# Two-layer transformer block on one core: k turned one head later in layer 0, masks of the maxima moved to VectorE and score pairs in layer 1

## The chip, the cores and the metric

The kernel runs on one core of one Trainium2 chip, in one launch. The metric is the device time in microseconds, the median of several executions. Engines are named as in the profile: PE is TensorE, DVE VectorE, ACT ScalarE, POOL GpSimd, SP SyncE (it issues the transfers).

## What is computed

Two layers follow each other on x of 1024 positions by 512 (32-bit floats). Each has an attention and a feed-forward part, each behind a layer norm with a scale and a shift from a small conditioning vector, and added to x through a gate. The change touches the two attentions. Cut to them:

```
# layer 0: 32 query heads, 8 k/v heads, head size 128, 4-bit weights
q, k, v = [((h @ ((qw - 8) * repeat(scales, 128, axis=0)))) ...]
q, k = q*cos + rotate_half(q)*sin, k*cos + rotate_half(k)*sin
scores = where(causal, q @ k.T / sqrt(128), min)
ctx = softmax(scores) @ v            # k, v of a group serve 4 heads
x += gate * (ctx @ dequantized(w_o))
# layer 1: 32 query heads, 8 k/v heads, head size 16
q, k = rope(q), rope(k)
scores = where(causal, q @ k.T / sqrt(16), -1e20)
x += gate * (softmax(scores) @ v @ w_o.T + b_o)
```

## The kernel before, in words

Constants, sizes: P is 128 partitions, S 1024 positions in NT = 8 tiles, two halves of HALF = 512 (TPH = 4 tiles each). 32-bit products are done on PE as products of a high and a low part in the format fp32r.

**Layer 0's attention** (`layer0_attention_phase`, line 350) goes through 256 units, 32 heads by 8 query tiles. PE's program is one loop over the units: the scores of the next unit, a part of the previous head's output product, partial products of the next head's q and, in every second unit, of the next group's k and v (`kv_partial`), the values, and the transposes of the probabilities. A group is 4 heads on one k and v; REP0 is 4. In a group's first head the partial products of the next group's k for positions 0 to 511 are made, in its second head those for 512 to 1023, then those of v. DVE adds the partial sums, and POOL applies the rotary embedding to each finished sum (`rope`, line 558 on: six instructions in order, the last at line 567 writes the low part). POOL's order is written out by hand (lines 612 to 618, and in the same order the list `pool_ropes`, lines 416 to 423, from which semaphore counts come). In head h: second half of q of head h, the o weights of head h (`make_o`, lines 591 to 600), first half of q of head h+1, and in two of four heads one half of k of the next group. PE waits for q's low part ahead of the first and the fifth query tile of a head, and for k's ahead of a group's first head; k has two places, by group.

The maximum of a row is taken on DVE in one custom instruction (line 768): it adds the table `keys_allowed` (0 or a large negative number) to the scores in PSUM, writes them back negated, and keeps the minimum; it is followed by a read of the accumulator.

**Layer 1's attention** (`layer1_attention_phase`, line 1341) goes by the 8 k/v groups of 4 heads of size 16. High and low parts of q and k lie stacked along the partitions, so one product gives a full-precision score. The scores are made twice. The y scores (queries on the partitions) of the group after only serve the maxima: `score_y` on PE, then `maximum` on DVE (line 1649), a plain maximum over at most 512 keys. The negated maxima are placed into the q stack, so that the x scores (keys on the partitions, `score_x`) come out with them subtracted; ACT takes the exponential (line 1712) into `probsT`, and `values` on PE (line 1583) multiplies with v. A piece on the diagonal is masked by a second, accumulating product of an identity and the bf16 tile `mem.causal` (line 1550 for x, 1569 for y). x has three PSUM banks, y three, the values one, and one bank serves all transposes ("staging": k line 1526, q line 1533, context line 1591), which DVE (k, context) or ACT (q) empties before the next use. A group has 48 x pieces (32 on the diagonal) and 48 y pieces (32 on the diagonal, widths 128, 256, 384 and 512 equally often).

The list `order` (lines 1365 to 1380) sets the program of every engine for one turn: x pieces 0 to 47 of a group, from the eighth on mixed with 6 y pieces of the next group for every 5, staging steps at fixed places, values one step behind. There are seven such turns; ahead of them stands a prologue with only the first group's y and staging steps (`order_first`), behind them the last group's x alone (`order_last`). DVE takes the k transposes of the next group out in two copies for each half (line 1642).

## Time and profile before

| what | value |
|---|---|
| runs | 1892.85, 1895.84, 1897.75 us; median 1895.84 |
| profiled execution, own time | 1891.85 us |
| its span | 1890.1 us |
| mean granted PE clock | 0.97 |
| busy, share of the span | PE 92%, DVE 61%, POOL 47%, ACT 43% |
| layer 0's attention | about 71 to 1044 us of the span |
| layer 1's attention | about 1385 to 1760 us |

The profile records one execution. Busy is the time in which an engine had an instruction under way; what it records of a matmul includes the way through the array, so that neighbours overlap. Idle time is given with what ended it. A timeline row with x2 or more is several like instructions in a row, with the time from the first start to the last end. The granted clock is 1.00 at 2.4 GHz and 0.50 at 1.2 GHz.

### The profile page before, as it was taken

The numbers are of one execution on the slowest core, as the hardware profiler recorded it, in microseconds if no ns is written. First come the engines' busy times: TensorE is split into PE (matmuls) and PEld (weight loads), VectorE is DVE, ScalarE is ACT, GpSimd is POOL, SyncE is SP. The second block draws the span as 40 slices with busy tenths as digits, with TensorE's granted clock in tenths as the row PEclk, the third lists the DMA queues.
The fourth block names the chain that finished last, engine by engine and source line by source line (L and its number), as shares of the span: only waits on it lengthen the run. The fifth ranks groups of instructions, "written<-read, shape, count | busy, mean of one in ns | idle before, by whom it ended". The sixth has DMA issues, their size and how long they took to land. (4 is left out here: it accounts for less than half of the span.)

```text
span 1890.1 us, 25001 instructions
## 1 busy us (share of the span) xinstructions
PE 1730.7 (92%) x9031; PEld 1264.5 (67%) x9031; DVE 1156.7 (61%) x2249; ACT 809.6 (43%) x1780; POOL 885.1 (47%) x784
## 2 busy tenths in 40 slices
PE   5699999999999999999999599998859999999778
PEld 3567777777777776777777388876735555555457
DVE  6856666566666575656655833345787666664475
ACT  3445454545445454545454221100315566566221
POOL 1686786876867868678774400000351222210200
PEclk9899999999999999999999899999879999999989
DMA  5101101010110110100100312102200000000021
GB/s 185 34 28 35 34 18 45 18 45 18 34 37 26 30 33 17 40 28 23 34 12 1 114 52 66 30 1 97 81 1 1 1 1 1 1 1 1 28 44 45
DMA packets 75315, 63.38 MB, mean 34 GB/s; under 512 B 23470, under 2 KB 53358, under 8 KB 75194
## 3 DMA queue, kind: packets, MB, share of 16 engines
q1 hardware_dynamic: 75194, 61.79, 11.0%
q8 instruction: 73, 1.20, 0.3%
q14 instruction: 48, 0.39, 0.1%
HBM read 59.68 MB, written 2.10 MB: 33 GB/s over the span
## 5 line engine op out<-in xcount | busy, mean ns | idle before, releaser
L844 ACT ACTIVATE a_probs<-psum,a_neg_max 128x128 f32<-128x128 f32 (+7 forms) x256 | 190.2, 743 | 265.3 <-DVE a_neg_max L768 265.0
L768 DVE CUSTOM_DVE_ANT_0 psum<-psum,a_keys_allowed 128x128 f32<-128x128 f32 (+7 forms) x256 | 195.4, 764 | 133.9 <-PE psum L77 133.7
L698 PE MATMUL psum<-a_probsT,a_v 128*128 128x512 f32 (+3 forms) x768 | 258.4, 486 | 0.2 <-ACT a_probsT L855 0.2
L1649 DVE TENSOR_REDUCE a_neg_max<-psum 128x1 f32<-128x512 f32 (+3 forms) x384 | 194.8, 553 | 97.2 <-PE psum L1569 62.6
L698 PEld LDWEIGHTS psum<-a_probsT,a_v 128*128 128x128 f32 x768 | 144.7, 190 | 117.3 <-issue 91.8
L1712 ACT ACTIVATE a_probsT<-psum 128x512 f32<-128x512 f32 (+3 forms) x384 | 173.3, 495 | 93.7 <-PE psum L1550 69.5
L780 DVE SCALAR_TENSOR_TENSOR x<-psum,a_row_inv,x 128x512 f32<-128x512 f32 x256 | 191.2, 749 | 16.9 <-PE psum L77 10.6
L785 DVE TENSOR_TENSOR a_ctxT_lo<-psum,a_ctxT_hi 128x512 fp32r<-128x512 f32 x64 | 44.3, 692 | 215.9 <-ACT a_ctxT_hi L861 215.9
L855 ACT COPY a_probsT<-psum 128x512 f32<-128x512 f32 (+3 forms) x384 | 171.0, 484 | 9.9 <-PE psum L685 9.8
L685 PE MATMUL psum<-ident,a_probs 128*128 128x128 f32 x1152 | 171.7, 274 | 0.4 <-ACT a_probsT L855 0.4
L75 PE MATMUL psum<-a_kT_hi,a_qT_lo 128*128 128x512 f32 (+3 forms) x384 | 150.6, 392 | 21.1 <-POOL a_qT_lo L567 21.1
L685 PEld LDWEIGHTS psum<-ident,a_probs 128*128 128x128 f32 x1152 | 138.7, 140 | 32.6 <-DVE x L780 4.7
L1547 PE MATMUL psum<-hT_hi,hT_lo 128*128 128x512 f32 (+3 forms) x384 | 150.3, 414 | 1.7 <-ACT a_probsT L1712 1.4
L558 POOL TENSOR_TENSOR a_turned_pool<-a_q_sum,a_sine 64x512 f32<-64x512 f32 x62 | 79.6, 1285 | 147.9 <-DVE a_q_sum L754 145.7
L1252 POOL TENSOR_TENSOR p_part<-p_qkv,p_rope 128x320 f32<-128x320 f32 x16 | 18.2, 1158 | 270.7 <-DVE p_qkv L1332 270.7
L754 DVE SCALAR_TENSOR_TENSOR a_q_sum<-psum,a_scale_q,a_q_sum 128x512 f32<-128x512 f32 x192 | 142.6, 743 | 0.6 <-ACT a_q_sum L832 0.2
L1566 PE MATMUL psum<-hT_lo,hT_hi 128*128 128x512 f32 (+3 forms) x384 | 138.2, 391 | 3.2 <-DVE a_neg_max L1649 1.3
L77 PE MATMUL psum<-a_kT_hi,a_qT_hi 128*128 128x512 f32 (+3 forms) x384 | 132.9, 346 | 0.0
L76 PE MATMUL psum<-a_kT_lo,a_qT_hi 128*128 128x512 f32 (+3 forms) x384 | 132.4, 345 | 0.0
L861 ACT CAST a_ctxT_hi<-psum 128x512 fp32r<-128x512 f32 x64 | 37.6, 587 | 213.8 <-PE psum L698 213.8
L649 PE MATMUL psum<-hT_lo,a_wq 128*128 128x512 f32 x256 | 102.0, 398 | 7.6 <-DVE a_k_sum L754 7.5
L1547 PEld LDWEIGHTS psum<-hT_hi,hT_lo 128*128 128x128 f32 x384 | 73.8, 194 | 52.0 <-ACT a_probsT L1712 42.2
(300 smaller groups left out, 4071.8 us busy)
## 6 DMA issues: line engine op xcount, KB each, us to landing
a_raw_q<-in_L_attn_qw_q SPq DMA_DIRECT2D x32, 256.0 KB, 4.0
a_raw_o<-in_L_attn_qw_o SPq DMA_DIRECT2D x32, 256.0 KB, 2.7
a_raw_scale_o<-in_L_attn_scales_o SPq DMA_DIRECT2D x32, 256.0 KB, 3.7
mod1b_w<-in_L_wmod SPq DMA_DIRECT2D x4, 1024.0 KB, 11.4
mod0a_w<-in_L_wmod SPq DMA_DIRECT2D x3, 1024.0 KB, 10.4
mod0b_w<-in_L_wmod SPq DMA_DIRECT2D x3, 1024.0 KB, 7.3
f_raw<-in_L_ffn_down_w SPq DMA_DIRECT2D x10, 256.0 KB, 3.1
f_raw<-in_L_ffn_gate_w SPq DMA_DIRECT2D x10, 256.0 KB, 3.3
```

Source lines behind the costliest of these rows:

```text
L75: pe.matmul(out, lhs_lo, rhs_hi, start=start, stop=False)
L685: last = nc.tensor.transpose(bank(use)[:, tile(j - c * TPH)], probs[:, u % 3, tile(j)], mem.ident[:, :])
L698: last = nc.tensor.matmul(bank(use)[:, first:HALF], v[:, g % 2, j, :], probsT[b][:, j, first:HALF], start=(j == 0), stop=(j == keys - 1))
L754: nc.vector.scalar_tensor_tensor(out=total, in0=bank(("part", key, k))[:, :], scalar=scale_of(key, k), in1=total, op0=ALU.mult, op1=ALU.ad ...
L768: nc.vector.tensor_tensor_reduce(out=scores, in0=scores, in1=keys_allowed[:, S - (i + 1) * P:S], scale=-1.0, scalar=-MASKED, op0=ALU.add, ...
L780: nc.vector.scalar_tensor_tensor(out=mem.x[:, t, :], in0=bank(use)[:, :], scalar=row_inv[:, h % 2, t:t + 1], in1=mem.x[:, t, :], op0=ALU.m ...
L844: nc.scalar.activation(probs[:, u % 3, 0:(i + 1) * P], score[u % 2][:, 0:(i + 1) * P], ACT.Exp, bias=neg_max[:, h % 2, i:i + 1], scale=-1. ...
L855: nc.scalar.copy(probsT[b][:, c * TPH:c * TPH + keys, tile(i % TPH)], bank(use)[:, 0:keys * P].rearrange("p (j q) -> p j q", j=keys)).then ...
L1547: last = nc.tensor.matmul(out[:, first:HALF], kB[:, h % 2, tile(j)], qB[:, h // 2, b * HALF + first:(b + 1) * HALF], start=True, stop=not ...
L1566: last = nc.tensor.matmul(out[:, 0:keys], qA[:, h // 2, tile(i)], kA[:, h % 2, c * HALF:c * HALF + keys], start=True, stop=not diagonal)
L1649: nc.vector.reduce_max(neg_max[:, c, i, h:h + 1], y_bank[n % SLOTS][:, 0:keys], AX.X, negate=True).then_inc(maxed.sem, 1)
L1712: nc.scalar.activation(probsT[:, s % SLOTS, h, first:HALF], x_bank[n % SLOTS][:, first:HALF], ACT.Exp).then_inc(exped.sem, 1)
```

## The change

It has three parts. In layer 0 POOL turns the two halves of the next group's k in the second and third head of a group and no longer in the first and second. In layer 1 the mask product of y goes: diagonal maxima use the custom instruction with a new table `allowed` of 128x512, which POOL clears and fills at the start and for which DVE waits once. And in layer 1 PE does the x pieces of two heads (even and odd) back to back where they lie on the diagonal, at the even one's place, then both masks.

```
--- before.py
+++ after.py
@@ -419,8 +419,8 @@
             pool_ropes.append(("q", h, 1))
         if h < LAST_HEAD:
             pool_ropes.append(("q", h + 1, 0))
-        if h % REP0 < 2 and h // REP0 < LAST_GROUP:
-            pool_ropes.append(("k", h // REP0 + 1, h % REP0))
+        if h % REP0 in (1, 2) and h // REP0 < LAST_GROUP:
+            pool_ropes.append(("k", h // REP0 + 1, h % REP0 - 1))
     dve_ropes = [("q", 0, 0), ("q", 0, 1)]
 
     with ExitStack() as ctx:
@@ -614,8 +614,8 @@
                 make_o(h)
                 if h < LAST_HEAD:
                     turn(("q", h + 1, 0))
-                if h % REP0 < 2 and h // REP0 < LAST_GROUP:
-                    turn(("k", h // REP0 + 1, h % REP0))
+                if h % REP0 in (1, 2) and h // REP0 < LAST_GROUP:
+                    turn(("k", h // REP0 + 1, h % REP0 - 1))
 
         @block.tensor
         def _(pe):
@@ -1400,6 +1400,7 @@
         probsT = sb("probsT", [P, SLOTS, REP1, HALF])
         ctxT = sb("ctxT", [P, HALF])
         neg_max, row_inv = sb("neg_max", [P, NHALF, NT, REP1]), sb("row_inv", [P, TPH, REP1])
+        allowed = sb("allowed", [P, HALF])
         cleared, filled = sem("cleared"), sem("filled")
 
         k_stacked, q_stacked = groups("k_stacked", ["k"]), groups("q_stacked", halves)
@@ -1429,11 +1430,11 @@
 
         @block.gpsimd
         def _(pool):
-            for buffer in (zero[:, :], k_stack[:, :, :, :]):
+            for buffer in (allowed[:, :], zero[:, :], k_stack[:, :, :, :]):
                 pool.memset(buffer, 0.0).then_inc(cleared, 1)
             for counter in (k_stacked, q_stacked, kB_begun, kB_made, v_made):
                 counter.open(pool)
-            pool.wait_ge(cleared, 2)
+            pool.wait_ge(cleared, 3)
 
             def from_group(group, width):
                 return bass.ds(group[0] * width + group[1] * width, width)
@@ -1488,10 +1489,12 @@
             stack_k((0, 0))
             for buffer in (q_stack[:, :, :, :], v[:, :, :]):
                 pool.memset(buffer, 0.0).then_inc(cleared, 1)
-            pool.wait_ge(cleared, 4)
+            pool.wait_ge(cleared, 5)
             pool.memset(v[:, :, HD1:HD1 + 1], 1.0).then_inc(cleared, 1)
-            pool.wait_ge(cleared, 5)
+            pool.wait_ge(cleared, 6)
             stack_q((0, 0), 0)
+            pool.affine_select(out=allowed[:, HALF - P:HALF], in_=allowed[:, HALF - P:HALF], compare_op=ALU.is_ge,
+                               fill=MASKED, base=0, pattern=[[-1, P]], channel_multiplier=1).then_inc(cleared, 1)
             stack_q((0, 0), 1)
             stack_k((0, 1))
             stack_q((0, 1), 0)
@@ -1536,20 +1539,27 @@
             def score_x(group, n):
 
                 b, j, h = xs[n]
+                if j < TPH * b:
+                    open_x(group, n, True).then_inc(x_scored.sem, 1)
+                elif h % 2 == 0:
+                    for m in (n, n + 1):
+                        open_x(group, m, False)
+                    for m in (n, n + 1):
+                        first = (j - TPH * b) * P
+                        nc.tensor.matmul(x_bank[m % SLOTS][:, first:first + P], mem.causal[:, :], mem.ident_bf[:, :],
+                                         start=False, stop=True).then_inc(x_scored.sem, 1)
+
+            def open_x(group, n, whole):
+
+                b, j, h = xs[n]
                 if (j, h) == (0, 0):
                     pe.wait_ge(*qB_out.now(group, (b, pairs[-1])))
                 if h == 0 and j == TPH * b:
                     pe.wait_ge(*kB_made.now(group, b))
                 pe.wait_ge(*(exped.now if n >= SLOTS else exped.last)(group, (n - SLOTS) % len(xs)))
                 first = max(0, j - TPH * b) * P
-                diagonal = j >= TPH * b
-                out = x_bank[n % SLOTS]
-                last = nc.tensor.matmul(out[:, first:HALF], kB[:, h % 2, tile(j)],
-                                        qB[:, h // 2, b * HALF + first:(b + 1) * HALF], start=True, stop=not diagonal)
-                if diagonal:
-                    last = nc.tensor.matmul(out[:, first:first + P], mem.causal[:, :], mem.ident_bf[:, :],
-                                            start=False, stop=True)
-                last.then_inc(x_scored.sem, 1)
+                return nc.tensor.matmul(x_bank[n % SLOTS][:, first:HALF], kB[:, h % 2, tile(j)],
+                                        qB[:, h // 2, b * HALF + first:(b + 1) * HALF], start=True, stop=whole)
 
             def score_y(group, n):
 
@@ -1561,14 +1571,8 @@
                     pe.wait_ge(*qA_out.now(group, (b, h // 2)))
                 pe.wait_ge(*(maxed.now if n >= SLOTS else maxed.last)(group, (n - SLOTS) % len(ys)))
                 keys = min(HALF, (i + 1) * P - c * HALF)
-                diagonal = c == b
-                out = y_bank[n % SLOTS]
-                last = nc.tensor.matmul(out[:, 0:keys], qA[:, h // 2, tile(i)],
-                                        kA[:, h % 2, c * HALF:c * HALF + keys], start=True, stop=not diagonal)
-                if diagonal:
-                    last = nc.tensor.matmul(out[:, keys - P:keys], mem.ident_bf[:, :], mem.causal[:, :],
-                                            start=False, stop=True)
-                last.then_inc(y_scored.sem, 1)
+                nc.tensor.matmul(y_bank[n % SLOTS][:, 0:keys], qA[:, h // 2, tile(i)],
+                                 kA[:, h % 2, c * HALF:c * HALF + keys], start=True, stop=True).then_inc(y_scored.sem, 1)
 
             def values(group, s):
 
@@ -1646,8 +1650,13 @@
                 h, i, c = ys[n]
                 dve.wait_ge(*y_scored.now(group, n))
                 keys = min(HALF, (i + 1) * P - c * HALF)
-                nc.vector.reduce_max(neg_max[:, c, i, h:h + 1], y_bank[n % SLOTS][:, 0:keys], AX.X,
-                                     negate=True).then_inc(maxed.sem, 1)
+                scores, neg = y_bank[n % SLOTS][:, 0:keys], neg_max[:, c, i, h:h + 1]
+                if c == i // TPH:
+                    nc.vector.tensor_tensor_reduce(out=scores, in0=scores, in1=allowed[:, HALF - keys:HALF], scale=-1.0,
+                                                   scalar=-MASKED, op0=ALU.add, op1=ALU.min, accum_out=neg
+                                                   ).then_inc(maxed.sem, 1)
+                else:
+                    nc.vector.reduce_max(neg, scores, AX.X, negate=True).then_inc(maxed.sem, 1)
 
             def place_maxima(group, b):
 
@@ -1688,6 +1697,7 @@
                     elif kind == "ctx":
                         normalize(own, *rest)
 
+            dve.wait_ge(cleared, 7)
             turn((0, -1), (0, 0), order_first)
             for g in range(0, LAST):
                 turn((g, 0), (g, 1), order)
```

**POOL, layer 0, in head 0** behind its o weights (a_wo_lo is the last of them; L558 to L567 are one rope, of q or of k). Before:

```order
L600 TENSOR_TENSOR a_wo_lo<-a_weight,a_wo_hi 128x512
L558 TENSOR_TENSOR a_turned_pool<-a_q_sum,a_sine 64x512
L559 TENSOR_TENSOR a_turned_pool<-a_q_sum,a_sine 64x512
L561 TENSOR_TENSOR a_q_sum<-a_q_sum,a_cosine 128x512
L563 TENSOR_TENSOR a_q_sum<-a_q_sum,a_turned_pool 128x512
L565 TENSOR_TENSOR a_qT_hi<-a_q_sum,a_zero 128x512
L567 TENSOR_TENSOR a_qT_lo<-a_q_sum,a_qT_hi 128x512
L558 TENSOR_TENSOR a_turned_pool<-a_k_sum,a_sine 64x512
L559 TENSOR_TENSOR a_turned_pool<-a_k_sum,a_sine 64x512
L561 TENSOR_TENSOR a_k_sum<-a_k_sum,a_cosine 128x512
L563 TENSOR_TENSOR a_k_sum<-a_k_sum,a_turned_pool 128x512
```

With the change, at the same place:

```order
L600 TENSOR_TENSOR a_wo_lo<-a_weight,a_wo_hi 128x512
L558 TENSOR_TENSOR a_turned_pool<-a_q_sum,a_sine 64x512
L559 TENSOR_TENSOR a_turned_pool<-a_q_sum,a_sine 64x512
L561 TENSOR_TENSOR a_q_sum<-a_q_sum,a_cosine 128x512
L563 TENSOR_TENSOR a_q_sum<-a_q_sum,a_turned_pool 128x512
L565 TENSOR_TENSOR a_qT_hi<-a_q_sum,a_zero 128x512
L567 TENSOR_TENSOR a_qT_lo<-a_q_sum,a_qT_hi 128x512
L558 TENSOR_TENSOR a_turned_pool<-a_q_sum,a_sine 64x512
L559 TENSOR_TENSOR a_turned_pool<-a_q_sum,a_sine 64x512
L561 TENSOR_TENSOR a_q_sum<-a_q_sum,a_cosine 128x512
L563 TENSOR_TENSOR a_q_sum<-a_q_sum,a_turned_pool 128x512
L565 TENSOR_TENSOR a_qT_hi<-a_q_sum,a_zero 128x512
```

The k rope between q's first half and q's second half is gone from head 0; it stands in the same gap one head later.

**PE, layer 1, first turn**, from a transposition of the q stack on (x products are hT_hi with hT_lo in this order, y products the other way round; ident_bf with causal masks x, causal with ident_bf masks y; a_probsT with a_v is a values step). Before:

```order
L1533 MATMUL psum<-ident,a_q_stack 128x128 x4
L1547 MATMUL psum<-hT_hi,hT_lo 128x256
L1550 MATMUL psum<-ident_bf,causal 128x128
L1566 MATMUL psum<-hT_lo,hT_hi 128x256
L1569 MATMUL psum<-causal,ident_bf 128x128
L1547 MATMUL psum<-hT_hi,hT_lo 128x256
L1550 MATMUL psum<-ident_bf,causal 128x128
L1566 MATMUL psum<-hT_lo,hT_hi 128x384
L1569 MATMUL psum<-causal,ident_bf 128x128
L1583 MATMUL psum<-a_probsT,a_v 32x384 x4
```

With the change:

```order
L1536 MATMUL psum<-ident,a_q_stack 128x128 x4
L1561 MATMUL psum<-hT_hi,hT_lo 128x256 x2
L1549 MATMUL psum<-ident_bf,causal 128x128 x2
L1574 MATMUL psum<-hT_lo,hT_hi 128x256
L1574 MATMUL psum<-hT_lo,hT_hi 128x384
L1587 MATMUL psum<-a_probsT,a_v 32x384 x4
```

Two x products stand together ahead of two masks, and the y products follow each other with no mask.

**DVE, layer 1**, maxima of the first group's second half with the change (before, all are TENSOR_REDUCE):

```order
L1659 TENSOR_REDUCE a_neg_max<-psum 128x1
L1655 ISA psum,a_neg_max<-psum,a_allowed 128x384
L1655 ISA a_neg_max 128x1
L1659 TENSOR_REDUCE a_neg_max<-psum 128x1
L1655 ISA psum,a_neg_max<-psum,a_allowed 128x512
L1655 ISA a_neg_max 128x1
```

Each diagonal maximum is now two instructions, the second of which writes the result.

## Rows read from the trace of the kernel before

**Rows 1.** Windows: us; PE, PEld, DVE, ACT, POOL busy (count); clock; DMA; GB/s
```profile
400.00:600.00 200.00, 195.60 (x948) 148.66 (x948) 124.91 (x236) 100.33 (x232) 149.24 (x121) 1.00 0.11 30
...
1500.00:1600.00 100.00, 94.79 (x697) 57.44 (x696) 67.64 (x142) 58.89 (x131) 22.33 (x33) 1.00 0.00 1
```

**Rows 2.** Groups by form, PE, 97 to 900: count | busy, mean ns | idle before, releaser
```profile
L75 PE MATMUL psum<-a_kT_hi,a_qT_lo 128*128 128x512 f32 x156 | 72.5, 465 | 21.1 <-POOL a_qT_lo L567 21.1
```

**Rows 3.** Timeline, POOL, layer 0: start, us, instruction, [idle before <- releaser]
```profile
171.26 1.29 POOL L558 TENSOR_TENSOR a_turned_pool<-a_q_sum,a_sine 64x512 f32<-64x512 f32 x1 [3.32 <-DVE a_q_sum L754]
...
185.08 1.30 POOL L558 TENSOR_TENSOR a_turned_pool<-a_q_sum,a_sine 64x512 f32<-64x512 f32 x1 [5.97 <-DVE a_q_sum L754]
...
201.45 1.29 POOL L558 TENSOR_TENSOR a_turned_pool<-a_q_sum,a_sine 64x512 f32<-64x512 f32 x1 [3.29 <-DVE a_q_sum L754]
...
213.46 1.29 POOL L558 TENSOR_TENSOR a_turned_pool<-a_k_sum,a_sine 64x512 f32<-64x512 f32 x1 [4.16 <-DVE a_k_sum L754]
...
221.36 1.26 POOL L558 TENSOR_TENSOR a_turned_pool<-a_q_sum,a_sine 64x512 f32<-64x512 f32 x1
...
227.84 1.27 POOL L567 TENSOR_TENSOR a_qT_lo<-a_q_sum,a_qT_hi 128x512 fp32r<-128x512 f32 x1
```

**Rows 4.** Timeline, PE, the first score of the fifth query tile
```profile
229.17 0.50 PE L75 MATMUL psum<-a_kT_hi,a_qT_lo 128*128 128x512 f32 x1 [1.47 <-POOL a_qT_lo L567]
```

**Rows 5.** Timeline, PE, layer 1, products with and without a mask
```profile
1535.86 0.39 PE L1566 MATMUL psum<-hT_lo,hT_hi 128*128 128x512 f32 x1
1536.09 0.39 PE L1547 MATMUL psum<-hT_hi,hT_lo 128*128 128x512 f32 x1
1536.32 0.22 PE L1566 MATMUL psum<-hT_lo,hT_hi 128*128 128x128 f32 x1
1536.39 0.23 PE L1569 MATMUL psum<-causal,ident_bf 128*128 128x128 bf16 x1
1536.42 0.47 PE L1547 MATMUL psum<-hT_hi,hT_lo 128*128 128x512 f32 x1
```

**Rows 6.** Groups by form, layer 1's attention, 1397 to 1760
```profile
L1649 DVE TENSOR_REDUCE a_neg_max<-psum 128x1 f32<-128x512 f32 x192 | 127.7, 687 | 41.2 <-PE psum L1566 30.0 <-PE psum L1569 10.4
...
L1569 PE MATMUL psum<-causal,ident_bf 128*128 128x128 bf16 x256 | 59.5, 232 | 0.0
```

**Rows 7.** Groups by form, layer 0, the masked maximum over 512 keys
```profile
L768 DVE CUSTOM_DVE_ANT_0 psum<-psum,a_keys_allowed 128x512 f32<-128x512 f32 x31 | 21.4, 690 | 0.0
```

**Rows 8.** Timeline, DVE, layer 0, around one accumulator read
```profile
601.23 0.14 DVE L768 DVE_READ_ACCUMULATOR2_ANT a_neg_max<- 128x1 f32 x1
601.23 0.75 DVE L780 SCALAR_TENSOR_TENSOR x<-psum,a_row_inv,x 128x512 f32<-128x512 f32 x1
601.89 0.74 DVE L754 SCALAR_TENSOR_TENSOR a_q_sum<-psum,a_scale_q,a_q_sum 128x512 f32<-128x512 f32 x1
```

**Rows 9.** Timeline, PE, the start of two turns of layer 1
```profile
1511.76 0.44 PE L1526 MATMUL psum<-ident,a_k_stack 128*128 128x128 f32 x2 [1.38 <-DVE attended L1671]
...
1555.32 0.66 PE L1526 MATMUL psum<-ident,a_k_stack 128*128 128x128 f32 x4 [1.38 <-DVE attended L1671]
```

**Rows 10.** Timeline, DVE and PE, the second half of the next k
```profile
1522.09 1.38 DVE L1642 CAST hT_lo<-psum 48x512 fp32r<-48x512 f32 x2
...
1523.93 0.28 PE L1533 MATMUL psum<-ident,a_q_stack 128*128 128x128 f32 x1
```

**Rows 11.** One window as in rows 1; timeline, DVE, 32 maxima of the first group
```profile
1378.00:1402.00 24.00, 6.64 (x29) 5.18 (x29) 16.25 (x22) 3.11 (x7) 11.96 (x18) 0.51 0.00 0
...
1408.74 16.02 DVE L1649 TENSOR_REDUCE a_neg_max<-psum 128x1 f32<-128x512 f32 x32
```

**Rows 12.** Timeline, POOL and DVE, the start of layer 1's attention
```profile
1391.76 0.61 POOL L1454 TENSOR_TENSOR a_q_stack<-q_hi,a_zero 128x256 f32<-128x256 f32 x1
...
1394.24 1.39 DVE L1642 CAST hT_lo<-psum 48x512 fp32r<-48x512 f32 x2 [1.27 <-issue]
```

**Rows 13.** Groups by form, ACT, layer 1's exponentials over 512 columns
```profile
L1712 ACT ACTIVATE a_probsT<-psum 128x512 f32<-128x512 f32 x192 | 106.4, 602 | 51.5 <-PE psum L1550 29.8 <-PE psum L1547 20.8
```

## Prediction

> **What bounds the kernel now.** I first read the busy table by stretch. In layer 0's attention TensorE (PE) is busy 195.60 us of 200 at granted clock 1.00, VectorE (DVE) 124.91, ScalarE (ACT) 100.33, POOL 149.24. In layer 1's attention PE has 94.79 of 100, DVE 67.64, ACT 58.89 [rows 1]. Both stages are PE's: time goes away where PE stops waiting or gets less to do, and the other engines matter only where PE waits for them.
>
> Then the groups of instructions, for what ends PE's idle time in layer 0. One group carries it: the first score product of a 512-key piece waits 21.1 us in all for the second part of a turned q, which POOL writes [rows 2]. The trace has 14 such stalls, two for each of the seven k/v groups made on the way; one is 1.47 us [rows 4].
>
> Then the timeline of POOL, for why POOL is late there. In a head without k work it was idle for 5.97 us when it took q's second half at 185.08. One head later the k rope stands ahead of that: it waits 4.16 us for its sum, runs from 213.46, and q's second half follows at 221.36, its last write starting at 227.84 [rows 3]. Two heads' first halves, each begun when its sum came, start 30.2 apart (171.26, 201.45) [rows 3]: a head's length. So the second half's sum was there at about 215.3, 30.2 after 185.08; the rope began 6.1 late, and PE lost 1.47: a margin of some 4.6 us.
>
> In layer 1 I read the timeline of PE for what a mask costs. Ends are start plus duration, rounded to 0.01. A 512-column product behind another unmasked one ends 0.23 us after it (1536.25 to 1536.48), the 128-column one 0.06 later, its mask 0.08 later, and the next 512-column product 0.27 to 0.28 later instead of 0.23 [rows 5]. So a mask is 0.075 of its own, and 0.05 more on the product behind it. The recorded 0.23 of a mask is mostly pipeline, no cost.
>
> **Layer 0: the k ropes one head later.** Nothing is added. The k rope now starts when its sum has been complete for about a head, right behind q's first half. In the head at 185 that would be near 179.1 (185.08 less 5.97 idle), and six instructions take 7.9 us (213.46 to 221.36) [rows 3]: to 187.0, so q's second half starts 2 us late. The margin is 4.6, so no stall. The o weights behind it also come 2 us late; they came 6 late before, without a PE stall on them. K is due at the first score of group g+1, two heads or more later. Its sum buffer and its place in kT are free as before. What remains late next is nothing that the non-k heads show. I take all 21.1 us; bounds 19 (each start refills the pipeline and finds small waits) and 21.5.
>
> **Layer 1, TensorE's part.** 256 masks on y (the score copy that only gives maxima) go [rows 6], 32 a group. By the order of the program, 14 of a group's 32 stand behind a product of 256 columns or more and ahead of another product, and give 0.075 + 0.05; the other 18 give 0.075 (ahead of a values step or a transpose, or behind a 128-column product, too short to cover the next weight load itself). That is 32 x 0.075 + 14 x 0.05 = 3.1 us a group.
>
> Pairs: 16 a group, 12 of 256 columns or more, where the second head's load now lies behind a product: 12 x 0.05 = 0.6. A mask behind a mask occurs nowhere. Lower bound: the bare spacing of 128 columns, 0.06 [rows 5]. Upper: two transposes of 128 columns take 0.44 and four 0.66 [rows 9], so 0.11 each. I take 0.075, since the mask costs the same behind a 128-column product, whose cover is as short; the upper bound costs 16 x 0.035 = 0.6 a group.
> The Trainium skill (TensorE: Matmul & The Clock Gate, LDWEIGHTS) says that a load takes its columns over 1.2 GHz whatever it loads, 107 ns here. The transposes' 0.11 agrees; the mask's 0.075 behind a short product doesn't. By the rule the pairs would give nothing and the total would be some 4 us less.
>
> **Layer 1, VectorE's part.** 256 plain maxima (687 ns recorded for 512 columns) [rows 6] become add, scale, minimum and write-back in one instruction plus a read of the accumulator. Layer 0 runs this pair: 690 ns for 512 columns [rows 7], so the body costs the same. The read lasts 0.14 us, but the next instruction has the same start as it, 601.23, and the one behind starts 0.66 later [rows 8]. So the read takes DVE about nothing from 0 to 0.14, but the result comes at its end: a bank of y is released 0.06 later. I take 0.015 per instruction.
> **What eats into it.** (a) A group's period ends with a DVE chain: the last four maxima, their placing and the normalization, for which PE waits 1.38 us before the k transposes, every 43.56 us [rows 9]. The chain grows by 0.1, and work moved ahead of it (head 1 of the first pair) or shortened inside it gives nothing: 0.3. (b) Two copies of k out of the staging bank occupy DVE for 1.38 us from 1522.09; PE came to the next use of that bank at 1523.93, 0.46 after their end [rows 10]. PE would now come 0.6 us earlier and wait, and then meet y banks held by the maxima queued behind the copies: 0.6. (c) The staging copies on ACT: 0.2. Sum 1.1 of 3.7, leaving 2.6 a group, bounds 1.2 and 3.7. Seven turns of this shape: 18.2 us.
>
> **Prologue and last group.** The first group's maxima are DVE's own pace: 32 in 16.02 us [rows 11]. 16 of them and 10 before get 0.015 longer, 0.4; the six ahead wait for masks that go, at the lower clock (0.51 from 1378 to 1402 [rows 11]) 0.15 each: -0.9. Together -0.5, bounds -1 and +4. POOL's new clear and mask fill are at most 1.3 us each, the row of an op over 128x512 [rows 3]. POOL's third copy into the q stack, behind which the fill is put, ends at 1392.37, and DVE first needs the fill at 1394.24 [rows 12]: with 2.6 us added, at worst 0.7 us late. The last group has no maxima; its 0.6 from pairs goes to exponentials of 602 ns that already lack work [rows 13]: 0, bounds -1 and +1.5.
>
> **Sum.** 21.1 + 18.2 + 0.5 = 39.8 off the profiled execution's own 1891.85 (span 1890.1): 1852. The median of the runs, 1895.84, stands 4.0 above that execution, so 1856.
>
> **Rivals.**
> (1) The accumulator read takes its 0.14 us of DVE. For: in layer 0 most reads stand ahead of another kind of instruction; in layer 1 pair follows pair. Against: rows 8. DVE gets 32 x 0.14 = 4.5 us more a group, mostly in the tight places: some 1.5 less saved in each of seven turns, and 26 x 0.14 = 3.6 in the prologue: 14 us, giving 1870. The Trainium skill (VectorE: DVE Perf Modes, The DRAIN you can't avoid) has this as its rule: each op empties the pipe first, so count of ops is what costs; here 256 more. The equal starts in layer 0 speak against it for this read.
> (2) Pairs starve on score banks. Three banks; a pair needs the exponential two back, and its first mask stands behind both products. For: a 512-column exponential is 602 ns [rows 13], and PE has little between some pairs. Against: values steps and y products of 0.5 to 1.1 us stand between most. At 0.15 us in each of 16 pairs, seven turns: 17 us, giving 1873.
> (3) Layer 0 gives nothing, another POOL-fed operand being late instead (q's second half late by more than 4.6). Against: 2 us by the rows. 1877.
> (4) Slower: DVE becomes the bound of layer 1. A turn has 43.56 us and DVE works some 29 of them [rows 1]. Layer 0's 21.1 is given back when a turn takes 3.0 longer, 46.6, which needs 17.6 us more DVE work, 0.55 per changed maximum, as if two PSUM streams in neighbouring banks halved its speed. At 0.8 a turn is 54.6, seven give +77, less 21: 1952.
>
> **How the numbers follow.** Forecast 0.68, (1) 0.13, (2) 0.10, (3) 0.05, (4) 0.02, no net change by a mixture of (2) and (3) 0.02. The forecast's own bounds are 1845 (all 3.7 a turn, 48 off, and the spread of runs) and 1866 (1.2 a turn). Reaching to 1870 takes in (1): 1845 to 1870. About 0.3%, 5.7 us, is what a measurement can tell from no change; all cases but the last two lie beyond it: faster 0.96, same 0.02, slower 0.02.
>
> **What would show it.** Right: no PE idle on POOL's q write in layer 0 and heads of equal length; layer 1 turns near 41.0 us; next instruction starting with the read; idle before the first staging use after k's second copies. Wrong: reads spaced 0.14 before their successor (rival 1); PE waiting on the exponential ahead of the pairs' second product (rival 2); a second mask 0.11 behind the first.

## The result, and the profile after

The changed kernel takes 1871.62 us (median of 4 runs, 1869.71 to 1872.44) against 1895.83 (4 runs): ratio 0.987, 95% interval 0.9855 to 0.9889. Faster, as forecast, but by 24.2 us instead of 39.8, and outside the range of 1845 to 1870. The profiled execution took 1872.44, its span is 1870.6.

The span in stages, each from the first instruction of PE named to that of the next stage. The clock is the mean granted clock of the stage; the last column is the term of the prediction.

| stage (until) | before | after | change | forecast |
|---|---|---|---|---|
| start (first product of layer 0's attention, the transposition of the scales) | 36.78 | 38.23 | +1.45 | 0 |
| layer 0's attention (last output product) | 1009.15 | 984.37 | -24.8 | -21.1 |
| feed-forward, layer 1's q, k, v (first k transpose) | 347.10, clock 0.91 | 348.79, 0.91 | +1.7 | 0 |
| layer 1's prologue (k transposes of the first turn) | 30.88, 0.84 | 32.55, 0.71 | +1.7 | -0.5 |
| seven turns | 303.74, 1.00 | 299.76, 0.98 | -4.0 | -18.2 |
| last group | 32.35, 1.00 | 34.20, 0.97 | +1.85 | 0 |
| layer 1's output and experts | 130.07, 0.93 | 132.72, 0.89 | +2.65 | 0 |

These sum to -19.5; in the medians it is -24.2, because the profiled execution of before lies 4.0 under its median and this one 0.8 over. The start runs the same instructions in every kernel here and took 36.1 to 38.4 in their profiles, so its 1.45 lies within what runs differ by.

Windows of the changed kernel, columns as in [rows 1]. In order: 200 us of layer 0, the prologue, one stretch at a turn's start, the turn after that one, which has such a stretch too, an undisturbed turn, and the output and experts:

```profile
377.00:577.00 200.00, 200.00 (x987) 154.22 (x986) 131.04 (x248) 106.44 (x243) 153.59 (x125) 1.00 0.11 31
1371.39:1403.94 32.55, 26.95 (x84) 17.08 (x85) 27.42 (x86) 3.51 (x6) 9.91 (x16) 0.71 0.00 0
1448.99:1452.40 3.41, 3.26 (x16) 1.62 (x16) 0.10 (x1) 1.79 (x4) 0.00 (x0) 0.50 0.00 0
1490.81:1534.71 43.90, 41.27 (x273) 24.13 (x273) 30.10 (x93) 25.94 (x58) 9.98 (x15) 0.96 0.00 1
1577.05:1619.40 42.35, 39.72 (x272) 23.65 (x273) 30.09 (x93) 25.84 (x58) 9.98 (x15) 1.00 0.01 1
1737.90:1870.62 132.72, 108.34 (x500) 81.44 (x500) 78.81 (x216) 27.08 (x55) 13.16 (x10) 0.89 0.17 42
```

The same windows of the kernel before, from the prologue on:

```profile
1393.03:1423.91 30.88, 25.63 (x114) 16.13 (x115) 25.24 (x53) 3.51 (x6) 9.19 (x14) 0.84 0.00 1
1511.76:1555.32 43.56, 41.67 (x304) 25.33 (x305) 29.22 (x61) 26.63 (x58) 9.98 (x15) 1.00 0.00 1
1760.00:1890.07 130.07, 104.74 (x500) 78.81 (x500) 78.88 (x216) 26.99 (x55) 13.17 (x10) 0.93 0.18 42
```

In layer 0, PE no longer stands still: 200.00 of 200 where [rows 1] had 195.60. Four undisturbed turns (the first, which takes 0.7 more in both kernels, and the three from 1534.71) are 1.21 to 1.22 us shorter than before. The other three hold a stretch of 3.41 us at granted clock 0.50 (a drop, below), and are 0.2 to 0.35 us longer than before, 1.5 longer than their neighbours. The turns of before had no such stretch.

Layer 0's stalls, by the groups of the changed kernel from 97 to 877, for [rows 2]:

```profile
L75 PE MATMUL psum<-a_kT_hi,a_qT_lo 128*128 128x512 f32 x156 | 72.1, 462 | 0.0
```

Two heads' first output products, a k rope's head between them, from the timelines of PE before (first fence) and after:

```profile
215.10 0.40 PE L75 MATMUL psum<-a_wo_hi,a_ctxT_lo 128*128 128x512 f32 x1
...
246.59 0.40 PE L75 MATMUL psum<-a_wo_hi,a_ctxT_lo 128*128 128x512 f32 x1
```

```profile
212.71 0.40 PE L75 MATMUL psum<-a_wo_hi,a_ctxT_lo 128*128 128x512 f32 x1
...
242.44 0.40 PE L75 MATMUL psum<-a_wo_hi,a_ctxT_lo 128*128 128x512 f32 x1
```

Such a head took 31.49 and takes 29.73, 1.76 less, though PE's recorded wait in it was 1.47 [rows 4]. Thirteen such heads (1.73 to 1.78 each) and the first, whose wait was 1.98 and which is 2.25 shorter, are the 24.8. So a stall of 1.47 cost 0.29 more than its recorded idle time. Most of that lies in how idle time is counted. PE around the stalled product, before (first fence; the product itself is [rows 4]) and after:

```profile
227.32 0.38 PE L685 MATMUL psum<-ident,a_probs 128*128 128x128 f32 x2
```

```profile
224.93 0.38 PE L685 MATMUL psum<-ident,a_probs 128*128 128x128 f32 x2
225.07 0.47 PE L75 MATMUL psum<-a_kT_hi,a_qT_lo 128*128 128x512 f32 x1
```

Without a wait the product starts 0.24 ahead of the recorded end of the transpositions (225.31). The 1.47 are counted from that end (227.70 to 229.17), so 0.24 has to be added to them.

The start of an undisturbed turn, PE, for [rows 9]:

```profile
1577.05 0.65 PE L1529 MATMUL psum<-ident,a_k_stack 128*128 128x128 f32 x4 [1.15 <-DVE attended L1680]
1577.46 0.71 PE L1561 MATMUL psum<-hT_hi,hT_lo 128*128 128x512 f32 x2
1578.02 0.28 PE L1549 MATMUL psum<-ident_bf,causal 128*128 128x128 bf16 x2
1579.19 0.66 PE L1536 MATMUL psum<-ident,a_q_stack 128*128 128x128 f32 x4 [0.89 <-DVE hT_lo L1646]
```

Piece 1 is now scored ahead of the k transposes, so the wait there is 1.15 instead of 1.38; but only one pair is left between k's and q's transposes, and that wait is 0.89 where it was 0.47. Two masks together take 0.28 where one takes 0.23 [rows 5]: a mask behind a mask costs 0.05. By the rule of the Trainium skill that the prediction set against this (TensorE: Matmul & The Clock Gate, LDWEIGHTS) it would be 0.107, which this row doesn't show. The weight loads of the same place (PEld):

```profile
1577.44 0.30 PEld L1561 LDWEIGHTS psum<-hT_hi,hT_lo 128*128 128x128 f32 x2
1578.01 0.12 PEld L1549 LDWEIGHTS psum<-ident_bf,causal 128*128 128x128 bf16 x2 [0.27 <-issue]
```

Two loads of 32-bit products are recorded at 0.30, two of bf16 masks at 0.12.

Three waits of loads in the second half of the same turn. In e2 below, without pairs, the first two don't occur and the third is 0.14:

```profile
1607.35 0.19 PEld L1561 LDWEIGHTS psum<-hT_hi,hT_lo 128*128 128x128 f32 x1 [0.32 <-ACT a_probsT L1722]
1610.75 0.19 PEld L1561 LDWEIGHTS psum<-hT_hi,hT_lo 128*128 128x128 f32 x1 [0.27 <-ACT a_probsT L1722]
1611.71 0.19 PEld L1574 LDWEIGHTS psum<-hT_lo,hT_hi 128*128 128x128 f32 x1 [0.36 <-DVE a_neg_max L1659]
```

The first two are of x pieces 37 and 41, second products of pairs, and PE's load waits for an exponential, as rival 2 says. The third is of y piece 41, whose bank a maximum holds.

DVE in a turn, two maxima and what follows them, for [rows 8]:

```profile
1596.98 0.42 DVE L1655 CUSTOM_DVE_ANT_0 psum<-psum,a_allowed 128x256 f32<-128x256 f32 x1
1597.32 0.14 DVE L1655 DVE_READ_ACCUMULATOR2_ANT a_neg_max<- 128x1 f32 x1
1597.32 0.68 DVE L1659 TENSOR_REDUCE a_neg_max<-psum 128x1 f32<-128x512 f32 x1
```

The accumulator read and the next maximum have one start. So it is with 142 of the 256 reads of layer 1; the instruction behind each of the other 114 waited for another engine or for a result that came later. Rival 1 falls: 256 more instructions lengthen nothing by themselves, and DVE's busy time grows by 0.9 us a turn (29.22 to 30.09), with the reads' 4.4 in it counted beside other work.

### The profile page after: what moved, and what is told of

Same layout as the page of the kernel before. It is cut to its first block and busy times, and to the rows that moved or that the text cites. A ratio compares the mean times of both kernels' runs of the same rounds, so it can differ in the third digit from the quotient of the medians.

```text
span 1870.6 us, 24749 instructions
## 1 busy us (share of the span) xinstructions
PE 1724.7 (92%) x8775; PEld 1258.4 (67%) x8775; DVE 1162.3 (62%) x2505; ACT 805.0 (43%) x1780; POOL 886.4 (47%) x786
## 5 line engine op out<-in xcount | busy, mean ns | idle before, releaser
L1722 ACT ACTIVATE a_probsT<-psum 128x512 f32<-128x512 f32 (+3 forms) x384 | 168.9, 493 | 92.4 <-PE psum L1549 72.8
L1655 DVE CUSTOM_DVE_ANT_0 psum<-psum,a_allowed 128x128 f32<-128x128 f32 (+3 forms) x256 | 123.2, 502 | 60.2 <-PE psum L1574 59.7
L558 POOL TENSOR_TENSOR a_turned_pool<-a_q_sum,a_sine 64x512 f32<-64x512 f32 x62 | 79.8, 1288 | 167.5 <-DVE a_q_sum L754 166.4
L1252 POOL TENSOR_TENSOR p_part<-p_qkv,p_rope 128x320 f32<-128x320 f32 x16 | 18.2, 1156 | 272.4 <-DVE p_qkv L1332 272.4
L1561 PE MATMUL psum<-hT_hi,hT_lo 128*128 128x512 f32 (+3 forms) x384 | 131.7, 395 | 4.1 <-ACT a_probsT L1722 3.7
L1574 PE MATMUL psum<-hT_lo,hT_hi 128*128 128x512 f32 (+3 forms) x384 | 125.8, 389 | 4.0 <-DVE a_neg_max L1655 1.4
L1561 PEld LDWEIGHTS psum<-hT_hi,hT_lo 128*128 128x128 f32 x384 | 65.9, 191 | 63.1 <-ACT a_probsT L1722 50.0
```

Of the source, the lines that this page charges most:

```text
L1561: return nc.tensor.matmul(x_bank[n % SLOTS][:, first:HALF], kB[:, h % 2, tile(j)], qB[:, h // 2, b * HALF + first:(b + 1) * HALF], start=T ...
L1722: nc.scalar.activation(probsT[:, s % SLOTS, h, first:HALF], x_bank[n % SLOTS][:, first:HALF], ACT.Exp).then_inc(exped.sem, 1)
```

## The experiments

"Turn" is an undisturbed one, from a k transpose to the next. The ratio is to the kernel before, measured beside each. All contain the layer 0 part.

**e1: the layer 0 part alone.** The two lines of the diff at `h % REP0`, nothing of layer 1.

> The layer 0 part alone. Both theories: the 14 stalls on POOL's low part of q are gone and nothing else changes, 21 us faster than before (0.9889 of it), layer 1's attention 367.0 us long as before, its turns 43.57, granted clock 1.00 through the turns. If instead the layer 0 part were what disturbs layer 1 (through where the clock stands when it begins), layer 1's attention would already be off here, and the ratio nearer 0.992.

1871.97 us, ratio 0.9878 (0.986 to 0.9897). Layer 0's attention takes 984.29, turns 43.57 at clock 1.00, prologue 30.90. So the layer 0 part gives all that the whole change gives, and layer 1's part, its gains and losses taken together, nothing. Its output and experts take 132.33 at clock 0.89, like the changed kernel's: the 2.3 us lost there against before belong to no part of layer 1's change.

**e2: with the masks of y on DVE, without pairs.**

Against the changed kernel, `score_x` is the one of before again:

```
-                if j < TPH * b:
-                    open_x(group, n, True).then_inc(x_scored.sem, 1)
-                elif h % 2 == 0:
...
+                diagonal = j >= TPH * b
...
+                if diagonal:
+                    last = nc.tensor.matmul(out[:, first:first + P], mem.causal[:, :], mem.ident_bf[:, :],
+                                            start=False, stop=True)
+                last.then_inc(x_scored.sem, 1)
```

> Layer 0 part and the masks of y on VectorE; x pieces one by one with their masks, as before. Theory P (the pairs give back what the masks brought): a turn of 41.3 to 42.0 us, no drop of the granted clock at turn starts, seven turns and the prologue together 12 us or more under the changed kernel, time 1855 to 1861. Theory D (VectorE's longer chain and the y banks eat the saving): a turn of 42.3 as in the changed kernel or more, time 1868 to 1875.

1862.65 us, ratio 0.9825 (0.9806 to 0.9844), 9 us under the changed kernel; the turn is 42.05. The time is 1.7 above theory P's range, and the granted clock does drop in its turns (three in the profiled execution, some 1.5 us each), so that part of P is wrong: drops don't need pairs. Of its four runs the profiled one was slowest (1867.39, clock 0.959); the others had 0.962 to 0.964.

Step for step against e1, by the ends of PE's instructions in a turn: 26 of the 32 masks that went give 0.07 each, and 13 products behind one 0.055 each, 2.6 us in all. Then 0.52 is lost around the first q transposes of the second half and the two y pieces behind them, 0.26 ahead of the context transposes, 0.16 at the turn's end and 0.17 in small pieces. PE, DVE and ACT of e2 at the first of these places:

```profile
1540.59 1.39 DVE L1639 CAST hT_lo<-psum 48x512 fp32r<-48x512 f32 x2
...
1542.01 0.57 DVE L1648 CUSTOM_DVE_ANT_0 psum<-psum,a_allowed 128x384 f32<-128x384 f32 x1
1542.03 0.66 PE L1536 MATMUL psum<-ident,a_q_stack 128*128 128x128 f32 x4
...
1542.60 0.69 DVE L1648 CUSTOM_DVE_ANT_0 psum<-psum,a_allowed 128x512 f32<-128x512 f32 x1
1542.73 0.39 PE L1567 MATMUL psum<-hT_lo,hT_hi 128*128 128x256 f32 x1
...
1543.40 0.75 PE L1567 MATMUL psum<-hT_lo,hT_hi 128*128 128x384 f32 x2
```

The q transposes start 0.05 behind the end of DVE's two copies, and the maxima that queued behind the copies (x384, x512) hold the y banks: the y product starts 0.67 after the one ahead of it.

**e3: the pairs alone, the masks of y on PE.** `score_x` and `open_x` of the change, `score_y` and `maximum` of before.

> Layer 0 part and the pairs; the masks of y stay on TensorE. Theory P: the pairs alone give nothing or cost, a turn of 43.3 to 44.5 us, last group 1 us longer, time 1873 to 1882 with PE waiting for exponentials ahead of second products. Theory D: the pairs give their 0.6 a turn, 43.0 us, time about 1870.

1875.34 us, ratio 0.9894 (0.9875 to 0.9914), 3.4 over e1. The turn is 43.43, 0.13 under e1 where the prediction wanted 0.6; the last group, of x alone, takes 33.7 for 32.3. Theory P's time, D's sign for the turn. Its prologue runs the instructions of e1's and takes 33.13 us at clock 0.76 (first fence), e1's 30.90 at 0.85 (second):

```profile
1370.11:1403.24 33.13, 28.14 (x117) 17.90 (x117) 26.65 (x56) 3.52 (x6) 9.21 (x14) 0.76 0.00 1
```

```profile
1369.20:1400.10 30.90, 25.57 (x115) 16.09 (x115) 25.25 (x53) 3.52 (x6) 9.22 (x14) 0.85 0.00 1
```

Two microseconds go or come in the prologue with the granted clock alone.

**e4: the changed kernel, pieces 0 and 1 not paired.**

```
-                if j < TPH * b:
+                if j >= TPH * b and not (n > 1):
+                    open_x(group, n, False)
+                    first = (j - TPH * b) * P
+                    nc.tensor.matmul(x_bank[n % SLOTS][:, first:first + P], mem.causal[:, :], mem.ident_bf[:, :],
+                                     start=False, stop=True).then_inc(x_scored.sem, 1)
+                elif j < TPH * b:
```

> The changed kernel, but the pieces 0 and 1 of a turn are not paired, so that x piece 1 stands behind the k transposes again, as before. Theory P, its part on the turn start: PE's wait ahead of the first q transposes falls from 0.89 to about 0.5 us, the drops of the granted clock at turn starts go, time 3 to 6 us under the changed kernel (1866 to 1869). Theory D: no change but the noise, 1871.

1865.31 us, ratio 0.9844 (0.9825 to 0.9862): 6.3 under the changed kernel. The wait ahead of the q transposes is 0.55, the one ahead of k's 1.45, no turn from the second on has a drop, and an undisturbed turn is 42.34 as in the changed kernel: the pull of piece 1 changes nothing in a clean turn, only where PE is idle. The pairs that are left cost 0.3 a turn against e2, and 1.15 in the last group (33.49 for 32.34). Three waits of that last group, PE, where e2 has none at these pieces:

```profile
1720.82 0.45 PE L1566 MATMUL psum<-hT_hi,hT_lo 128*128 128x384 f32 x1 [0.40 <-ACT a_probsT L1727]
1723.67 0.38 PE L1566 MATMUL psum<-hT_hi,hT_lo 128*128 128x256 f32 x1 [0.35 <-ACT a_probsT L1727]
1725.94 0.33 PE L1566 MATMUL psum<-hT_hi,hT_lo 128*128 128x128 f32 x1 [0.30 <-ACT a_probsT L1727]
```

They are second products of pairs, waiting for the exponential two back, as in rival 2. In a turn e4's loads wait at the same places as the changed kernel's (0.32 and 0.27 for exponentials, 0.36 for a maximum); set against e2 by the ends, 0.22 is lost from y piece 33 to 36, across pair 36, and 0.24 from y piece 38 to 41.

**e5: e2 with pairs only in the first half** (e4's condition, with `1 < n < TPH * REP1`).

> e2 (masks of y on VectorE, x pieces one by one) with pairs only for x pieces 2 to 15, the ones of the first half. In e4 these pairs brought PE 0.2 us by piece 11 and none by the first q transposes of the second half, where PE waits for the staging bank and the y banks. Theory A (pairs of the first half are swallowed there, those of the second half, at pieces 32 to 47, are what costs): turn 42.05 us as in e2 within 0.08, last group 30.4 to 30.9 us, time that of e2 (1862.7) but for the number of clock drops, each 1.5 us. Theory B (every pair costs alike): turn 42.2, last group 31.0 or more.

1863.26 us, ratio 0.982 (0.9796 to 0.9844). Turn 42.05, as in e2: theory A. (The last group's 30.4 to 30.9 in that text set out from a wrong base; e2's is 32.34, e5's 32.7.) First-half pairs give nothing, and the 0.3 a turn comes from pieces 32 to 47. Its profile has three drops too; two turns with one took 42.93, 0.85 longer and not 1.5.

**e6: e2 with PE's idle times at a turn's start filled.**

`fill(group, n, times)` waits for the bank of x piece n as its product does, and makes that product so many times.

```
+                        if of_order is order and step == ("kA", 0):
+                            fill(own, 1, 4)
+                        elif of_order is order and step == ("qA", 0, 0):
+                            fill(own, 4, 2)
                         wait_stage_bank(own, following, step, of_order)
```

> e2 with useless products in PE's two idle times at a turn's start: the product of x piece 1 four times before the k transposes, that of piece 4 twice before the first q transposes (overwritten by the real ones). Theory C (the drops of the granted clock at turn starts come from PE standing idle there, whoever makes it idle): the turns have clock 1.00 throughout, none is longer than 42.1 us, turns together 4.5 us shorter than e2's, time 1857 to 1859. Rival (the drops come from elsewhere, or filler delays the transposes): drops in the turns stay, or turns of 42.3 and more, time 1862 or above.

1864.23 us, ratio 0.9824 (0.98 to 0.9849): a miss in time, no faster than e2. In the profile the theory's part holds: every turn is 42.01 to 42.07 at clock 1.00, the first six 252.3 us where e2's took 255.7. Its prologue took 33.69 for e2's 32.24. What drops cost e2's median can't be told from this; e13 asks it of the changed kernel, where all four runs had a clock of 0.958 or 0.959.

**e7: e2 with one of the two k copies on ACT.**

```
+            def take_k1(group, b):
+                act.wait_ge(*kA_turned.now(group, b))
+                act.wait_ge(*kB_made.last(group, b))
+                rows = slice(STACK, STACK + USED)
+                nc.scalar.copy(kA[rows, 1, half(b)], stage_bank[rows, :]).then_inc(kA_out.sem, 1)
...
-                for n in range(2):
-                    rows = slice(n * STACK, n * STACK + USED)
-                    last = nc.vector.tensor_copy(kA[rows, n, half(b)], stage_bank[rows, :])
-                last.then_inc(kA_out.sem, 1)
+                rows = slice(0, USED)
+                nc.vector.tensor_copy(kA[rows, 0, half(b)], stage_bank[rows, :]).then_inc(kA_out.sem, 1)
```

`take_k1` is ACT's; each half of k now counts two on `kA_out`.

> e2 with the second of the two copies of k out of the staging bank done on ACT instead of DVE. Theory D (DVE's 1.38 us of copies are what holds the staging bank and then the y banks, where the masks' saving is lost: 0.47 us ahead of the first q transposes, 0.5 about those of the second half): both go, turn 41.2 to 41.5 us, time 1857 to 1860. Rival (y banks are short for another reason, and ACT pays): turn 41.8 or more, time 1861 or above.

1853.61 us, ratio 0.9771 (0.9748 to 0.9795), 9.0 under e2. The window of its turn:

```profile
1522.86:1563.93 41.07, 39.21 (x272) 23.48 (x272) 28.74 (x91) 27.33 (x60) 9.98 (x15) 1.00 0.00 1
```

Theory D is borne out, turn and time: DVE works 1.4 us less a turn, ACT 0.9 more, and PE no longer waits ahead of the first q transposes nor in the second half; what is left is 1.53 at the turn's start and 0.20 at the context transposes. No turn from the second on had a drop, and its prologue is 29.59.

**e8: e2 with the staging steps later.**

```
-    at = {1: [("kA", 0)], 4: [("qA", 0, 0)], 6: [("qB", 1, 0)], 8: [("qB", 1, 1)], 10: [("qA", 0, 1)], 12: [("kA", 1)],
-          15: [("qA", 1, 0)], 17: [("qA", 1, 1)], 20: [("ctx", 0)], 25: [("qB", 0, 0)], 27: [("qB", 0, 1)]}
+    at = {3: [("kA", 0)], 6: [("qA", 0, 0)], 8: [("qB", 1, 0)], 10: [("qB", 1, 1)], 12: [("qA", 0, 1)], 14: [("kA", 1)],
+          17: [("qA", 1, 0)], 19: [("qA", 1, 1)], 22: [("ctx", 0)], 25: [("qB", 0, 0)], 27: [("qB", 0, 1)]}
-    FIRST_Y = 7
+    FIRST_Y = 8
```

> e2 with the k transposes put behind x piece 2 and the staging steps after them some 2 pieces later each, so that x pieces 1 and 2 lie in the wait for DVE's chain and the next three and a values step between k's transposes and q's. Theory E (the waits at the turn's start are latency that any work covers): of 2.0 us idle there 1.0 or more goes, turn 41.0 to 41.3 us, no clock drops in the turns, time 1854 to 1859. Rival (the waits move on to the q transposes and y pieces behind): turn 42 or more, time 1861 or above.

1862.1 us, ratio 0.9817 (0.9792 to 0.9841), turn 42.05: the rival. The wait at the turn's start fell to 0.82, but 0.42 came back behind k's copies, 0.18 on an exponential ahead of the first values step, 0.18 on ACT's q copy, 0.14 and 0.07 at y banks. No drops in its turns; its output and experts took 130.14 at clock 0.93, as before the change.

**e9 to e12, on one chip** (the kernel before took 1892.77 there, 1896.40 beside e7, so they are compared with e7 by their turns). e9 is e7 with pairs but the first, e10 e7 with first-half pairs, e12 e7 with e8's table; e11 is e2 with this (`score_one` is e2's `score_x`, a product and its mask):

```
+                if n < 2 * TPH * REP1:
+                    score_one(group, n)
+                elif n % 2 == 0:
+                    score_one(group, n)
+                    score_one(group, n + 1)
```

> e7 (masks of y on VectorE, k's copies split between DVE and ACT, 1853.6 us, turn 41.07) with pairs for all diagonal x pieces but 0 and 1. Theory A (first-half pairs do save PE 0.2 us but it was swallowed by the waits that e7 took away; second-half pairs starve on exponentials and cost 0.3): turn 41.1 to 41.3, last group 1 us longer, time 1854 to 1857. Rival (with DVE's copies out of the way all pairs pay): turn 40.6 to 40.8, time 1850 to 1852.

1858.05 us, ratio 0.9812 (0.9795 to 0.9828). Turn 41.47: pairs cost 0.4 of it, more than A said; the rival is out.

> e7 with pairs only for x pieces 2 to 15. Theory A: the 0.2 us is kept now, turn 40.85 to 40.95, last group as in e7, time 1851.5 to 1853. Rival (swallowed again by another wait): turn 41.05, time 1853.6.

1853.63 us, ratio 0.9791 (0.9773 to 0.9808). Turn 41.23, 0.16 over e7 and longer than both texts have it, though the time is the rival's. By the ends, the pairs had given 0.15 when piece 11 was done; 0.07 of it went at the second half's k transposes, 0.08 at the pair 12 and 13 (128 columns), and 0.19 more at the second half's second q transposes. In no run do pairs shorten a turn by more than e3's 0.13.

> e2 (1862.7, clean turn 42.05, last group 32.34) with the second-half diagonal x pieces 32 to 47 two by two at the even one's place, but each product with its own mask right behind it, so that the first exponential need not wait for the second product. Theory F (what costs in a pair is that the first mask, and so its exponential and so the bank two pieces on, comes a product later): turn 42.05 to 42.15, last group 32.3, time 1862 to 1864. Rival G (it is the two pieces being asked for at once that outruns the exponentials): turn 42.3 and last group 33 or more, as with the pairs, time 1865 to 1867.

1864.44 us, ratio 0.9848 (0.9831 to 0.9865). Turn 42.45, last group 32.32. Each theory has one of two: in the last group, where only x pieces run, own masks take the whole cost away (F); in a turn, asking for two pieces together costs 0.4 even so (G).

> e7 with e8's table (k transposes behind x piece 2, the staging steps some two pieces later). In e8 the wait at the turn's start fell from 1.53 to 0.82 us but 0.42 came back behind k's copies in the second half, 0.19 at the second half's own q and 0.5 at exponentials. Theory H (the copies' part of that goes with the split): turn 40.2 to 40.6, time 1847 to 1851. Rival (exponentials and staging copies on ACT now set the pace there): turn 41 or more, time 1853 or above.

1855.96 us, ratio 0.9798 (0.9781 to 0.9816). Turn 41.46, the rival: PE's waits are 0.82 at the turn's start, 0.48 on an exponential ahead of the first values step, 0.18 on ACT's q copy. ACT has become what is waited for.

**e13: the changed kernel with the idle times filled** (e6's edit, with piece 2 in place of 1).

> The changed kernel itself, with useless products in PE's two idle times at a turn's start (the product of x piece 2 four times, that of piece 4 twice, overwritten by the real ones). Theory C (the drops of the granted clock in its turns come from PE standing idle there, and cost it about 1.5 us each): all turns 42.3 to 42.4 us at clock 1.00, the seven turns together 3 to 5 us shorter than the changed kernel's 299.8, time 1867 to 1869. Rival (the drops in the turns are chance and cost little in the median): time 1871 to 1873.

1867.42 us, ratio 0.9856 (0.984 to 0.9873): 4.2 under the changed kernel, as theory C has it; in the profile the seven turns are 5.6 shorter, 0.8 of that in the first. 254 us of its turns and one of them, columns as above:

```profile
1402.25:1656.25 254.00, 246.84 (x1670) 147.37 (x1669) 180.66 (x558) 156.25 (x351) 60.04 (x90) 1.00 0.00 1
1529.18:1571.50 42.32, 41.06 (x279) 24.54 (x279) 30.11 (x93) 25.83 (x58) 10.00 (x15) 1.00 0.01 1
```

More work for PE, and less time, as three drops of 1.5 would have it (all four runs are below all four of the changed kernel). That PE's standing idle is what brings the drops fits this, but is not proved by it: e4 has no drop either, with nothing filled and waits of 1.45 and 0.55.

**e14: the changed kernel with e7's split.**

> The changed kernel with the second copy of k on ACT instead of DVE, and nothing else. Theory D: the copies hold it as they hold e2, so it gains nearly what e2 gained (9 us) less the pairs' cost, which can't be hidden any more: turn 41.4 to 41.7, time 1859 to 1863. Rival (in the changed kernel the pairs are the larger cost and the copies matter little): turn 42.0 or more, time 1868 or above.

1857.68 us, ratio 0.9802 (0.9786 to 0.9819), 13.9 under the changed kernel; turn 41.48 with no drop. Theory D, its time just better than said. The waits at exponentials and at y piece 41 are still there.

**e15: e7 with pairs at 32, 34, 38 and 42 only.**

> e7 with pairs only for x pieces 32, 34, 38 and 42, the ones of the second half that have a values step of 1 us between them and the pair before. Set against e2 by the ends of PE's instructions, e4 gained 0.07 to 0.08 us at each of these and lost 0.11 to 0.23 at 36, 40 and 44, which follow a pair without a values step. Theory G (a pair pays its load where the exponential two back has had a values step's time, and starves where not): turn 40.75 to 40.9 us, time 1851.5 to 1853. Rival (a pair never pays, its first exponential comes late everywhere): turn 41.1 or more, time 1854 or above.

1855.19 us, ratio 0.9787 (0.9771 to 0.9803). Turn 41.41, 0.35 over e7 (one of its turns had a drop and took 42.65): theory G falls, and so does the rival's reason. By the ends, these pairs do give their 0.08 each, the first two 0.18; the loss comes behind them, at y pieces 35 (0.36) and 41 (0.25). PE's loads (PEld) at the first of these:

```profile
1556.65 0.19 PEld L1579 LDWEIGHTS psum<-hT_lo,hT_hi 128*128 128x128 f32 x1 [0.45 <-DVE a_neg_max L1662]
```

and DVE and PE ahead of it:

```profile
1555.39 0.53 PE L1579 MATMUL psum<-hT_lo,hT_hi 128*128 128x512 f32 x2
...
1555.90 0.69 DVE L1662 TENSOR_REDUCE a_neg_max<-psum 128x1 f32<-128x512 f32 x1 [0.92 <-PE psum L1579]
...
1556.51 0.29 DVE L1658 CUSTOM_DVE_ANT_0 psum<-psum,a_allowed 128x128 f32<-128x128 f32 x1
```

The load at 1556.65 is that of y piece 35, which takes the bank of piece 32. With both x pieces at the even one's place, piece 32 comes later: DVE stands idle for 0.92 waiting for it (0.71 in e7) and begins its maximum at 1555.90, 0.6 us of work. Pieces 33 to 35 then follow more closely than before. Drawing two pieces of one ring together bunches those of the other ring behind them.

## Why the prediction was wrong

- **Layer 0: right in kind, small in size.** All 14 stalls went, none came in their place. The term was 21.1 with an upper bound of 21.5; it measured 24.8, since a stall costs 1.76 and not the 1.47 of idle time recorded (the first 2.25 and not 1.98).
- **Layer 1, the masks of y: right in kind, a sixth too large.** 3.1 a group was forecast from 0.075 a mask and 0.05 behind 14 of them; 0.07 from 26 masks and 0.055 from 13 products make 2.6 (e2 against e1).
- **"What eats into it", 1.1 a turn: right.** e2 lost 1.1: 0.16 for (a), 0.52 for (b) and 0.26 for (c), forecast at 0.3, 0.6 and 0.2, and 0.17 elsewhere. e7 shows (b) by taking its cause away: 1.0 of a turn goes, the 0.47 ahead of the first q transposes with it. Its profile has no drop in the turns from the second on either; of the six kernels with that split e9 and e15 have one.
- **Layer 1, the pairs: wrong, and this is the step that failed.** "12 x 0.05 = 0.6" a group priced the loads that a neighbour hides, which indeed are hidden, and nothing of the order of the work. By itself a pair did pay 0.07 to 0.08: 0.05 of load and 0.025 because a mask behind a mask costs 0.05 and not the 0.075 taken. But pairs gave 0.13 a turn in e3 and cost 0.3 to 0.4 on top of the masks' change (e4, e9), and 1.15 in the last group. That is rival 2 in the last group (waits on the exponential two back) and in a turn also: the loads of x pieces 37 and 41 wait 0.32 and 0.27 for exponentials. The prediction had weighed this and let it go, since values steps and y products stand between most pairs; pairs 36 and 40 follow one without a values step. Beside it stands the wait at y piece 41's bank, which no rival named, and e15 shows that y banks alone suffice: without the waits on exponentials its pairs still lose 0.35. With 2.6 less 1.1 less 0.3, a turn saves the 1.2 measured.
- **The granted clock: not in the sum at all.** The turns of before are at 1.00, and I left it there. Three of the changed kernel's turns had a drop at their start, about PE's two idle times of 1.15 and 0.89 us, and were 1.5 us longer for it; e13 fills these and gives 4.2 us back. The prologue (+1.7) and the output and experts (+2.65) ran at a lower clock than before. For the last stage e1 and e8, 132.3 and 130.1 with the same instructions, show that this comes with the clock and not with the work. For the prologue e3 and e1, the same instructions at clock 0.76 and 0.85, show that the clock alone can bring 2.2; how much of the changed kernel's 1.7 is its doing was not measured, and e4, the same but for the first pair, took 32.06 at clock 0.71, 0.5 less. What makes the clock fall in one kernel's prologue and not in another's stays open: e2 and e4 wait equally long at a turn's start (2.00 and 1.99 us), and the profile of e2 has drops in its turns and e4's has none; e3 and e11, with waits like these, had one each; e9 and e15, with the wait ahead of the q transposes gone, had one each, e7, e10 and e14, with it gone or at 0.2, had none from the second turn on.
- **The sum.** A turn saved 1.4 less than forecast, seven times: 9.7. Drops in the turns: 4.5. Prologue and last group: 4.0. Start, middle and last stage: 5.8. Layer 0: -3.7. Together 20.3, by which the profiled execution missed its 1852 (1872.4). The medians differ by less, 15.6.

Rival 2, at 1873 and with a tenth of the chance, comes nearest in time. Its mechanism was there, but not its size: it asked for 17 us of waits, and the pairs' own cost was 0.3 in each of seven turns and 1.15 in the last group. That the times agree to 1.4 us is luck, and the range was cut off at rival 1's 1870, below it.

**The better version** is e7 (e10's 1853.63 equals it, with a turn 0.16 longer, on a chip where the kernel before took 3.6 less): masks of y on DVE, no pairs, k's copies split, 1853.61 us, 0.977 of before and 18.0 us under the changed kernel.

## What to carry to other kernels

Price a change of order by the rings of buffers on both sides of it: a pair that saves 0.08 us on a load and a mask had its own second product wait 0.3 for an exponential, or moved a y piece behind it and lost 0.36 at a bank. Where an engine waits twice for one queue, moving one item off that queue (0.7 us of copy to an engine with time) gave 1.0 us a turn, where 32 instructions less on the bound engine had given 1.5 of their 2.6. And where the granted clock is 1.00, don't take for granted that it stays there: the changed kernel's turns lost 4.5 us to three stretches at 0.50 that the kernel before had not.

## What the runs showed of the hardware

- A mask product of 128 columns in bf16 behind another costs 0.05 us (0.28 for two, 0.23 for one), less than the 0.075 that it costs between 32-bit products. Two such masks' loads are recorded at 0.12, two of 32-bit products at 0.30.
- A wait of 1.47 us on PE ahead of a product cost 1.76 from head to head, thirteen times alike, 0.24 of the difference because the next product would have started before the recorded end of the last.
- Useless products made a kernel faster: 6 more a turn and 4.2 us less in all, with the granted clock at 1.00 in all its turns (e13). In e6, with such products too, nothing was gained in time.
- A stretch of 3.41 us at granted clock 0.50 cost a turn 1.5 us in the changed kernel and in e2 and 0.85 in e5.
- The accumulator read of the custom maximum and the next instruction have one start 142 times of 256 in layer 1 (the other 114 times the next one waited for something else), and the read takes nothing from DVE's pace there. The Trainium skill (VectorE: DVE Perf Modes, The DRAIN you can't avoid) has the next instruction wait until the pipe is empty, but lets one that is not held start earlier; of these reads the rows show the latter.
